# V projected and sent out ahead of Q and K in each of a kernel's eight attentions

## The chip, the core and the metric

The kernel runs on one core of a Trainium2 chip. The metric is the device time of one execution in microseconds (us); less is better. The five engines of the core run their own instruction streams and wait for each other on semaphores: TensorE (PE, matmuls), VectorE (DVE), ScalarE (ACT), GpSimd (POOL) and SyncE (SP), which here only issues DMAs. ACT issues DMAs as well.

## What is computed

Eight sequences of 512 tokens with 128 features go through four residual blocks, each behind a layer norm:

```python
x = x + ssm(layernorm(x))          # depthwise conv, state-space scan over time
x = x + ffn(layernorm(x))          # 8 experts, all computed, mixed by two softmaxes
x = x + attention(layernorm(x))    # below
x = x + ffn(layernorm(x))          # the same weights again

# attention: 16 heads of 8 features, chunk 10, left context 25
q = (x @ Wq.T + bq) * scaling;  k = x @ Wk.T + bk;  v = x @ Wv.T + bv
scores = q @ k.T + chunk_mask
out = softmax(scores) @ v
out = out @ Wo.T + bo
```

A query sees only its own chunk of 10 tokens and 25 to the left, so scores are computed for windows of 30 queries and 64 keys.

## The kernel before

**The beat.** The expert network is the bulk of the work. It is cut into 512 chunks (16 passes over a sequence, 32 chunks each; a chunk is 128 hidden features of one expert). In chunk `c` PE computes the gate projection `pg` (3 matmuls of 128x512, one line each of `split3`), the up projection `pu` of chunk `c-1` (3 more), and the down projections `pd` (line 994) of chunk `c-4` and its neighbours; ACT applies SiLU to `pg` (line 1049), DVE multiplies by `pu` (line 1087) and adds each finished expert into `x` (line 1075, "weigh").

**The side work.** The other blocks of other sequences are slipped between the chunks. Each is a generator per engine that yields the chunk at which its next piece is due, and `interleave` writes the pieces into that engine's stream in this order. A whole number is due after the chunk's `pg` and `pu` and ahead of its `pd`, a half number behind `pd`. So the order on each engine is fixed when the program is built, and the engines meet only at semaphores. `T_ATT[j] = 38 + 55 * j` is the chunk at which attention `j` begins, `T_SSM` holds the slots of the state-space blocks.

**An attention before its first scores.** PE transposes the normed rows (slot `t0 + 4`), ACT and DVE split them into two parts `axh`, `axl`. Then PE projects Q and K (slot 6, three matmuls of 128x512 each), and later V (slot 7.5, twelve matmuls of 128x128). They go to two PSUM banks in turn (`att_ps`): `take` waits until the bank's last user has freed it. ACT writes the high part of Q and K (line 720, slot 6.5), DVE the low part (line 754, slot 7), which frees the bank. DVE copies V into a padded layout `staged` (line 764, sixteen copies, slot 8), which frees V's bank.

**The DMAs of an attention, all in SP's queue** (q1 in the profile), in this order before the change:
- four stores of Q and K, high and low, to `qk_rows` in DRAM (line 836, 256 KB each), each behind its own producer;
- eight loads back into `q3` and `k3` in a regrouped layout (line 842, 256 KB each), each behind its store's landing;
- one store of V to `v_rows` (line 849, 1024 KB);
- eight gathers of V for the first half of the windows (line 863, 144 or 128 KB each, in pieces of 512 bytes), behind the landing of the V store; eight more for the second half, behind the scores of unit 1.

POOL builds the query weights for the first scores (line 886). It waits for all eight loads, for V's bank and for the V store:

```python
pool.wait_ge(qk_moved, 16 * 8 * (j + 1))
ab.wait_free(pool, ("v", j))
pool.wait_ge(v_out, 16 * (j + 1))
```

PE's first scores (line 676, slot `13.5 + 1/8`) wait for POOL's first two query weights, and everything behind them in PE's stream waits too.

**The state-space block's DMAs go through ACT's queue** (q10): per block eight loads of 256 KB (`arena<-bc_spread`, lines 607 and 611), each of which spreads 2 rows of DRAM over 128 partitions. POOL (lines 628, 632) uses them. Attentions 0, 2 and 4 have such loads in flight while their own DMAs run; the others have none at that point, or only at its end.

Of the kernel before, what the change touches and what calls it, by code (L numbers as in the profile page):

```python
# [8 lines left out]
F32 = mybir.dt.float32  # L9
# [4 lines left out]
B, L, D = 8, 512, 128  # L14
# [67 lines left out]
def build(nc, x_d, pack_d, wg_d, wu_d, wd_d, out_d):  # L82
    ctx = contextlib.ExitStack()
    with ctx:
# [558 lines left out]
        class Att:  # L643
# [9 lines left out]
            def pe(pe, link, j):  # L653
# [4 lines left out]
                ab.wait_free(pe, ("ln3", j))  # L658
                for w, name in ((wq, ("q", j)), (wk, ("k", j))):
                    ps = ab.take(pe, name)  # L660
                    ab.fill(split3(ps[:, :], [v[:, :] for v in w], (axh[:, 0:L], axl[:, 0:L])), name)
                yield t0 + 7.5
                ps = ab.take(pe, ("v", j))
                for t in range(TT):
# [3 lines left out]
                    last = nc.tensor.matmul(out, xw[0], wv[1][:, :], start=False, stop=True)  # L668
                ab.fill(last, ("v", j))

                def scores(n):
# [40 lines left out]
            def act(act, link, j):  # L712
# [3 lines left out]
                nc.scalar.copy(axh[:, 0:L], ab.ps(("ln3", j))[:, :]).then_inc(x_hi, 1)  # L716
                yield t0 + 6.5
                for w, v in enumerate("qk"):
# [21 lines left out]
            def dve(dve, link, j):  # L740
# [10 lines left out]
                yield t0 + 7  # L751
                for w, v in enumerate("qk"):
                    dve.wait_ge(qk_hi, 2 * j + w + 1)
                    ab.free(nc.vector.scalar_tensor_tensor(qk_s[:, w, 1, :], ab.ps((v, j))[:, :], pk("b_" + v),
                                                           qk_s[:, w, 0, :].bitcast(F32), ALU.add, ALU.subtract), (v, j))
                yield t0 + 8
                ab.wait(dve, ("v", j))
# [3 lines left out]
                for t in range(TT):  # L761

                    for r in range(4):
                        ins = nc.vector.tensor_copy(v_s[:, t, r, :].rearrange("p (g h d) -> p g h d", g=4, d=HD)[:, :, r, :],
                                                    ab.ps(("v", j))[:, t * P:(t + 1) * P]
                                                    .rearrange("p (g h d) -> p g h d", g=4, d=HD)[:, :, r, :])
                        if (t, r) == (TT - 1, 3):
                            ab.free(ins, ("v", j))
                        else:
                            link.count(ins)  # L770

                def masked(n):
# [49 lines left out]
            def sp(sp, link, j):  # L822


                qk_r = qk_d[j % 2]
                yield T_ATT[j] + 7
                if j >= 2:
                    sp.wait_ge(qk_moved, 16 * 8 * (j - 1))
                for w, v in enumerate("qk"):
                    for part in range(2):  # L830
                        yield T_ATT[j] + 7 + 0.5 * w
                        if part == 0:
                            sp.wait_ge(qk_hi, 2 * j + w + 1)
                        else:
                            ab.wait_free(sp, (v, j))
                        sp.dma_start(qk_r[w, part], qk_s[:, w, part, :].bitcast(F32)).then_inc(qk_out[w][part], 16)
                yield T_ATT[j] + 8
                for w, (dst, parts) in enumerate(((q3, (0, 0, 1, 1)), (k3, (0, 1, 0, 1)))):
                    for i, part in enumerate(parts):
# [3 lines left out]
                                     qk_r[w, part].rearrange("(g e) l -> e g l", g=4)).then_inc(qk_moved, 16)  # L843

                yield T_ATT[j] + 9
                if j:
                    sp.wait_ge(v_moved[1], 16 * 8 * j)
                ab.wait_free(sp, ("v", j))
                sp.dma_start(v_d[LEFT:LEFT + L, :].rearrange("(t p) x -> p t x", p=P), u_b[:, :, :]).then_inc(v_out, 16)

# [373 lines left out]
```

## Time and profile before

| | us |
|---|---|
| three runs | 1535.48, 1539.36, 1539.65 (median 1539.36) |
| the profiled execution, its own time | 1539.28 |
| its span from first to last instruction | 1537.5 |
| busy in it: PE | 1428.3 (93%) |
| DVE | 1000.8 (65%) |
| ACT | 791.9 (52%) |
| POOL | 459.5 (30%) |

Times in the rows are microseconds from the start of the span. "busy" counts instructions only, not waits and not the issuing of DMAs. Brackets behind a row of the timeline give how long the engine had stood idle before it and what released it. PEclk is the granted TensorE clock as a share of full speed (2.4 GHz); 0.50 is 1.2 GHz. "DMA share" is the mean busy share of the core's 16 DMA engines, so that 0.125 is what two busy engines make.

### The profile page before, as it was taken

The numbers are of one execution on the slowest core, as the hardware profiler recorded it, in microseconds if no ns is written. First come the engines' busy times: TensorE is split into PE (matmuls) and PEld (weight loads), VectorE is DVE, ScalarE is ACT, GpSimd is POOL, SyncE is SP. The second block draws the span as 40 slices with busy tenths as digits, with TensorE's granted clock in tenths as the row PEclk, the third lists the DMA queues.
The fourth block names the chain that finished last, engine by engine and source line by source line (L and its number), as shares of the span: only waits on it lengthen the run. The fifth ranks groups of instructions, "written<-read, shape, count | busy, mean of one in ns | idle before, by whom it ended". The sixth has DMA issues, their size and how long they took to land.

```text
span 1537.5 us, 27266 instructions
## 1 busy us (share of the span) xinstructions
PE 1428.3 (93%) x10580; PEld 1227.8 (80%) x10580; DVE 1000.8 (65%) x2317; ACT 791.9 (52%) x1114; POOL 459.5 (30%) x416
## 2 busy tenths in 40 slices
PE   5789957999999989999999899999999999999998
PEld 3577846887888878788788788887888888888887
DVE  5655636777587666866876577658756776486543
ACT  6462723855467445674656456465742555366321
POOL 4342253234232342223621354115512221141000
PEclk9999977999999999999999899999999999999999
DMA  5110142001601151014200520034004200420000
GB/s 171 45 47 23 55 139 45 15 16 49 155 1 36 45 141 25 2 43 151 45 8 10 169 47 22 1 129 83 28 1 132 44 1 2 138 38 2 1 7 8
DMA packets 82076, 81.57 MB, mean 53 GB/s; under 512 B 4748, under 2 KB 55948, under 8 KB 81948
## 3 DMA queue, kind: packets, MB, share of 16 engines
q1 hardware_dynamic: 74444, 64.92, 15.8%
q10 hardware_dynamic: 7504, 14.91, 2.7%
q8 instruction: 84, 1.38, 0.4%
q14 instruction: 44, 0.36, 0.1%
HBM read 60.65 MB, written 19.17 MB: 52 GB/s over the span
## 4 chain that ended last, share of the span: by engine, by line
PE 69%; DVE 11%; DMA 7%; issue 5%; ACT 5%; POOL 3%; SPq 1%; ACTq 0%; DVEq 0%; POOLq 0%
PE pd L994 23%; PE pg L270 7%; PE pu L270 6%; PE pg L272 6%; PE pg L271 6%; PE pu L271 6%; PE pu L272 6%; DMA arena<-bc_spread 3%; PE att_ps L676 3%; DVE h L1087 2%; PE att_ps L698 1%; DMA v_rows<-staged 1%; DVE x L1075 1%; DMA att_arena<-v_rows 1%; DVE att_arena L798 1%
## 5 line engine op out<-in xcount | busy, mean ns | idle before, releaser
L1049 ACT ACTIVATE h<-pg 128x512 f32<-128x512 f32 x512 | 304.0, 598 | 631.2 <-PE pg L272 620.6
L994 PEld LDWEIGHTS pd<-w_down,h 128*128 128x128 f32 x4096 | 513.7, 193 | 31.1 <-issue 3.9
L994 PE MATMUL pd<-w_down,h 128*128 128x128 f32 x4096 | 533.2, 279 | 1.1 <-DVE x L1075 1.1
L1087 DVE TENSOR_TENSOR h<-h,pu 128x512 f32<-128x512 f32 x512 | 344.0, 676 | 207.2 <-PE pu L272 206.1
L270 PE MATMUL pg<-ffn_x_hi,w_gate_hi 128*128 128x512 f32 x512 | 246.2, 481 | 5.4 <-ACT h L1049 3.9
L270 PE MATMUL pu<-ffn_x_hi,w_up_hi 128*128 128x512 f32 x512 | 208.2, 407 | 27.4 <-DVE h L1087 27.3
L271 PE MATMUL pu<-ffn_x_lo,w_up_hi 128*128 128x512 f32 x512 | 205.5, 401 | 0.0
L271 PE MATMUL pg<-ffn_x_lo,w_gate_hi 128*128 128x512 f32 x512 | 205.4, 401 | 0.0
L272 PE MATMUL pg<-ffn_x_hi,w_gate_lo 128*128 128x512 f32 x512 | 205.0, 400 | 0.0
L272 PE MATMUL pu<-ffn_x_hi,w_up_lo 128*128 128x512 f32 x512 | 204.8, 400 | 0.0
L899 POOL TENSOR_TENSOR att_arena<-att_arena 128x512 f32<-128x512 f32 (+1 forms) x72 | 73.8, 1025 | 352.9 <-DVE att_arena L789 352.9
L886 POOL TENSOR_TENSOR q_weights<-q,pack 128x512 fp32r<-128x512 f32 x136 | 145.1, 1088 | 102.6 <-DMA v_rows<-staged 102.5
L1049 ACT ACT_TABLE_LOAD x124 | 159.1, 1283 | 8.4 <-issue 6.2
L1075 DVE SCALAR_TENSOR_TENSOR x<-pd,mix,x 128x128 f32<-128x128 f32 x512 | 143.5, 342 | 22.2 <-PE pd L994 18.1
L270 PEld LDWEIGHTS pu<-ffn_x_hi,w_up_hi 128*128 128x128 f32 x512 | 97.8, 191 | 59.8 <-DVE h L1087 36.9
L272 PEld LDWEIGHTS pg<-ffn_x_hi,w_gate_lo 128*128 128x128 f32 x512 | 98.3, 192 | 24.1
L272 PEld LDWEIGHTS pu<-ffn_x_hi,w_up_lo 128*128 128x128 f32 x512 | 97.9, 191 | 24.2
L271 PEld LDWEIGHTS pu<-ffn_x_lo,w_up_hi 128*128 128x128 f32 x512 | 98.1, 192 | 22.8
L270 PEld LDWEIGHTS pg<-ffn_x_hi,w_gate_hi 128*128 128x128 f32 x512 | 99.9, 195 | 13.3 <-ACT h L1049 5.0
L271 PEld LDWEIGHTS pg<-ffn_x_lo,w_gate_hi 128*128 128x128 f32 x512 | 99.9, 195 | 4.8 <-issue 1.4
L676 PEld LDWEIGHTS att_ps<-k,q_weights 128*128 128x128 f32 x544 | 74.3, 199 | 27.6 <-issue 21.9
L676 PE MATMUL att_ps<-k,q_weights 128*128 128x64 f32 x544 | 70.7, 274 | 20.6 <-POOL q_weights L886 20.6
(189 smaller groups left out, 1472.6 us busy)
## 6 DMA issues: line engine op xcount, KB each, us to landing
arena<-bc_spread ACTq DMA_DIRECT2D x56, 256.0 KB
att_arena<-v_rows SPq DMA_DIRECT2D x64, 144.0 KB, 4.0
qk_rows<-qk_parts SPq DMA_DIRECT2D x32, 256.0 KB, 3.0
q<-qk_rows SPq DMA_DIRECT2D x32, 256.0 KB, 3.7
k<-qk_rows SPq DMA_DIRECT2D x32, 256.0 KB, 4.7
v_rows<-staged SPq DMA_DIRECT2D x8, 1024.0 KB, 8.5
att_arena<-v_rows SPq DMA_DIRECT2D x64, 128.0 KB, 4.1
arena<-in_x SPq DMA_DIRECT2D x8, 256.0 KB, 2.9
```

What stands on the lines that cost most here:

```text
L270: nc.tensor.matmul(out, w[0], x_parts[0], start=first, stop=False)
L271: nc.tensor.matmul(out, w[0], x_parts[1], start=False, stop=False)
L272: return nc.tensor.matmul(out, w[1], x_parts[0], start=False, stop=last)
L676: last = nc.tensor.matmul(ps[:, (4 * i + g) * WK:(4 * i + g + 1) * WK], q_w[:, n % 2, i, g, :, :].rearrange("p r q -> p (r q)"), k3[:, g, ...
L698: last = nc.tensor.matmul(ps[32 * g:32 * g + 32, i * QW:(i + 1) * QW], v_w[:, w, v, 32 * g:32 * g + 32], pt[n % 2][:, i, g, v, :], start=( ...
L798: link(nc.vector.tensor_tensor(u, u, rs.unsqueeze(3).broadcast_to([P, nw, 4, WK]), ALU.mult))
L886: nc.gpsimd.tensor_tensor(q_w[:, n % 2, i, :, :, :], q3[:, :, w * WQ:w * WQ + QW].bitcast(F32).unsqueeze(2) .broadcast_to([P, 4, 4, QW]), ...
L899: nc.gpsimd.tensor_tensor(u, u, smax[:, 0:nw, :].unsqueeze(3).broadcast_to([P, nw, 4, WK]), ALU.subtract).then_inc(s_sub, 1)
L994: last = nc.tensor.matmul(pd[:, t * P:(t + 1) * P], h_b[:, d % NH, t * P:(t + 1) * P], wd[:, d % NCH, :], start=d % CPE == 0 and t == 0, s ...
L1049: nc.scalar.activation(h_b[:, c % NH, :], pg[c % 2][:, :], ACT.Silu).then_inc(gate_done, 1)
L1075: nc.vector.scalar_tensor_tensor(x[:, t, :], pd[:, t * P:(t + 1) * P], mix[m % 2][:, t, e % E:e % E + 1], x[:, t, :], ALU.mult, ALU.add).t ...
L1087: nc.vector.tensor_tensor(h, h, pu[d % 2][:, :], ALU.mult).then_inc(h_done, 1)
```

## The change

In each attention V now goes first. On PE the twelve V matmuls stand at slot 6 and Q and K at slot 7. DVE's copies of V stand at slot 7 and its low parts of Q and K at slot 8; ACT's high parts move from 6.5 to 7.5. In SP's queue the store of V stands ahead of the stores and loads of Q and K. No instruction is added, removed or resized, and no semaphore that anyone waits for is changed. POOL's code and order are the same.

```diff
@@ PE
                 ab.wait_free(pe, ("ln3", j))
-                for w, name in ((wq, ("q", j)), (wk, ("k", j))):
-                    ps = ab.take(pe, name)
-                    ab.fill(split3(ps[:, :], [v[:, :] for v in w], (axh[:, 0:L], axl[:, 0:L])), name)
-                yield t0 + 7.5
                 ps = ab.take(pe, ("v", j))
...
                 ab.fill(last, ("v", j))
+                yield t0 + 7
+                for w, name in ((wq, ("q", j)), (wk, ("k", j))):
+                    ps = ab.take(pe, name)
+                    ab.fill(split3(ps[:, :], [v[:, :] for v in w], (axh[:, 0:L], axl[:, 0:L])), name)
@@ ACT
-                yield t0 + 6.5
+                yield t0 + 7.5
                 for w, v in enumerate("qk"):
@@ DVE
                 yield t0 + 7
-                for w, v in enumerate("qk"):
-                    dve.wait_ge(qk_hi, 2 * j + w + 1)
-                    ab.free(nc.vector.scalar_tensor_tensor(qk_s[:, w, 1, :], ab.ps((v, j))[:, :], pk("b_" + v),
-                                                           qk_s[:, w, 0, :].bitcast(F32), ALU.add, ALU.subtract), (v, j))
-                yield t0 + 8
                 ab.wait(dve, ("v", j))
...
+                yield t0 + 8
+                for w, v in enumerate("qk"):
+                    dve.wait_ge(qk_hi, 2 * j + w + 1)
+                    ab.free(nc.vector.scalar_tensor_tensor(qk_s[:, w, 1, :], ab.ps((v, j))[:, :], pk("b_" + v),
+                                                           qk_s[:, w, 0, :].bitcast(F32), ALU.add, ALU.subtract), (v, j))
@@ SP
+                yield T_ATT[j] + 7
+                if j:
+                    sp.wait_ge(v_moved[1], 16 * 8 * j)
+                ab.wait_free(sp, ("v", j))
+                sp.dma_start(v_d[LEFT:LEFT + L, :].rearrange("(t p) x -> p t x", p=P), u_b[:, :, :]).then_inc(v_out, 16)
                 qk_r = qk_d[j % 2]
-                yield T_ATT[j] + 7
+                yield T_ATT[j] + 8
...
-                yield T_ATT[j] + 9
-                if j:
-                    sp.wait_ge(v_moved[1], 16 * 8 * j)
-                ab.wait_free(sp, ("v", j))
-                sp.dma_start(v_d[LEFT:LEFT + L, :].rearrange("(t p) x -> p t x", p=P), u_b[:, :, :]).then_inc(v_out, 16)
```

The order of SP's issues around attention 0; the rows with a minus are those of before (line 849 is the V store), those with a plus those of the change (line 830 is the V store, 842 the stores and 848 the loads of Q and K).

```order
 L913 DMA arena<-in_x 128x4x128
 L917 DMA x<-in_x 128x4x128
-L836 DMA qk_rows<-qk_parts 128x512 x4
-L842 DMA q<-qk_rows 32x4x512 x4
-L842 DMA k<-qk_rows 32x4x512 x4
-L849 DMA v_rows<-staged 128x4x512
+L830 DMA v_rows<-staged 128x4x512
+L842 DMA qk_rows<-qk_parts 128x512 x4
+L848 DMA q<-qk_rows 32x4x512 x4
+L848 DMA k<-qk_rows 32x4x512 x4
 L863 DMA att_arena<-v_rows 32x8x128 x8
 L913 DMA arena<-in_x 128x4x128
```

The V store has passed twelve other DMAs, and the last thing in front of the gathers is now a load of K instead of the store of V.

The order on PE in attention 1, first of before, from K's projection to the first two V matmuls:

```order
L270 MATMUL att_ps<-attn_x,w_k_hi 128x512
L271 MATMUL att_ps<-attn_x,w_k_hi 128x512
L272 MATMUL att_ps<-attn_x,w_k_lo 128x512
L994 MATMUL pd<-w_down,h 128x128 x4
L270 MATMUL pg<-ffn_x_hi,w_gate_hi 128x512
L271 MATMUL pg<-ffn_x_lo,w_gate_hi 128x512
L272 MATMUL pg<-ffn_x_hi,w_gate_lo 128x512
L270 MATMUL pu<-ffn_x_hi,w_up_hi 128x512
L271 MATMUL pu<-ffn_x_lo,w_up_hi 128x512
L272 MATMUL pu<-ffn_x_hi,w_up_lo 128x512
L666 MATMUL att_ps<-w_v_hi,attn_x 128x128
L667 MATMUL att_ps<-w_v_hi,attn_x 128x128
```

and of the change at the same place, from the last V matmul to K's first:

```order
L664 MATMUL att_ps<-w_v_lo,attn_x 128x128
L994 MATMUL pd<-w_down,h 128x128 x4
L270 MATMUL pg<-ffn_x_hi,w_gate_hi 128x512
L271 MATMUL pg<-ffn_x_lo,w_gate_hi 128x512
L272 MATMUL pg<-ffn_x_hi,w_gate_lo 128x512
L270 MATMUL pu<-ffn_x_hi,w_up_hi 128x512
L271 MATMUL pu<-ffn_x_lo,w_up_hi 128x512
L272 MATMUL pu<-ffn_x_hi,w_up_lo 128x512
L270 MATMUL att_ps<-attn_x,w_q_hi 128x512
L271 MATMUL att_ps<-attn_x,w_q_hi 128x512
L272 MATMUL att_ps<-attn_x,w_q_lo 128x512
L270 MATMUL att_ps<-attn_x,w_k_hi 128x512
```

V has taken the place of Q and K, and Q and K stand one chunk's `pd`, `pg` and `pu` behind it. The second bank used after V is Q's; K comes back to V's.

The order on DVE at the same attention, with the high parts of Q and K awaited by lines 754 (before) and 769 (change):

```order
 L1087 TENSOR_TENSOR h<-h,pu 128x512 x2
 L1075 SCALAR_TENSOR_TENSOR x<-pd,mix,x 128x128 x4
-L754 SCALAR_TENSOR_TENSOR qk_parts<-att_ps,pack,qk_parts 128x512 x2
-L1087 TENSOR_TENSOR h<-h,pu 128x512
-L764 COPY staged<-att_ps 128x4x8 x16
+L759 COPY staged<-att_ps 128x4x8 x16
+L1087 TENSOR_TENSOR h<-h,pu 128x512
+L769 SCALAR_TENSOR_TENSOR qk_parts<-att_ps,pack,qk_parts 128x512 x2
```

The sixteen copies and the two low parts have changed places around one product of the expert network.

## Rows read from the trace of the kernel before

**Rows 1.** The page: busy time of each engine

```profile
PE 1428.3 (93%) x10580; PEld 1227.8 (80%) x10580; DVE 1000.8 (65%) x2317; ACT 791.9 (52%) x1114; POOL 459.5 (30%) x416
```

**Rows 2.** Waits over the whole span: us in total, times, longest us

```profile
PE att_ps L676 <- POOL q_weights L886: 20.6, 3, 9.3
POOL q_weights L886 <- DMA v_rows<-staged: 102.5, 6, 29.9
```

**Rows 3.** Timeline of SP's DMA issues, attention 2: start, us, line, tile, count

```profile
534.04 2.07 SPq L836 DMA_DIRECT2D qk_rows<-qk_parts  x4
...
544.88 0.64 SPq L849 DMA_DIRECT2D v_rows<-staged  x1
556.26 20.65 SPq L863 DMA_DIRECT2D att_arena<-v_rows  x16
```

**Rows 4.** Timeline of POOL and PE at the first scores, attentions 2 and 4

```profile
556.40 2.04 POOL L886 TENSOR_TENSOR q_weights<-q,pack 128x512 fp32r<-128x512 f32 x2 [10.11 <-DMA v_rows<-staged]
...
558.58 1.89 PE L676 MATMUL att_ps<-k,q_weights 128*128 128x64 f32 x8 [4.62 <-POOL q_weights L886]
...
875.80 3.51 POOL L886 TENSOR_TENSOR q_weights<-q,pack 128x512 fp32r<-128x512 f32 x2
...
879.45 1.89 PE L676 MATMUL att_ps<-k,q_weights 128*128 128x64 f32 x8 [6.67 <-POOL q_weights L886]
```

**Rows 5.** Windows: stretch, length, busy us of each engine, PEclk, DMA share, GB/s

```profile
484.00:488.00 4.00, 4.00 (x54) 3.27 (x54) 3.51 (x8) 3.46 (x5) 2.34 (x2) 1.00 0.13 49
...
552.00:556.00 4.00, 1.96 (x11) 1.34 (x10) 0.00 (x0) 1.84 (x3) 0.00 (x0) 1.00 0.14 54
...
871.00:875.00 4.00, 1.78 (x10) 1.16 (x8) 0.00 (x0) 0.60 (x1) 0.57 (x1) 1.00 0.13 51
```

**Rows 6.** Timeline of SP's DMA issues, attention 6

```profile
1171.44 2.09 SPq L836 DMA_DIRECT2D qk_rows<-qk_parts  x4
...
1180.27 0.54 SPq L849 DMA_DIRECT2D v_rows<-staged  x1
1186.45 3.79 SPq L863 DMA_DIRECT2D att_arena<-v_rows  x8
```

**Rows 7.** Windows of attention 6: its stores and loads, then the gathers

```profile
1173.00:1185.00 12.00, 12.00 (x81) 10.79 (x80) 8.47 (x36) 3.44 (x7) 2.52 (x3) 1.00 0.95 325
...
1187.00:1193.00 6.00, 6.00 (x43) 5.45 (x43) 2.49 (x8) 1.87 (x3) 3.64 (x4) 1.00 0.95 176
```

**Rows 8.** Timeline of POOL and PE at the first scores, attentions 5, 6 and 7

```profile
1033.17 4.04 POOL L886 TENSOR_TENSOR q_weights<-q,pack 128x512 fp32r<-128x512 f32 x4 [29.89 <-DMA v_rows<-staged]
...
1035.58 0.97 PE L676 MATMUL att_ps<-k,q_weights 128*128 128x64 f32 x8
...
1192.21 0.97 PE L676 MATMUL att_ps<-k,q_weights 128*128 128x64 f32 x8
...
1333.82 4.04 POOL L886 TENSOR_TENSOR q_weights<-q,pack 128x512 fp32r<-128x512 f32 x4 [25.77 <-DMA v_rows<-staged]
...
1336.80 0.97 PE L676 MATMUL att_ps<-k,q_weights 128*128 128x64 f32 x8
```

**Rows 9.** Timeline of PE and DVE around the projections, attentions 1 and 0

```profile
378.52 0.40 PE L270 MATMUL att_ps<-attn_x,w_k_hi 128*128 128x512 f32 x1
...
379.22 1.05 PE L994 MATMUL pd<-w_down,h 128*128 128x128 f32 x8
...
380.31 1.13 DVE L1075 SCALAR_TENSOR_TENSOR x<-pd,mix,x 128x128 f32<-128x128 f32 x4 [1.54 <-PE pd L994]
...
382.15 0.33 PE L666 MATMUL att_ps<-w_v_hi,attn_x 128*128 128x128 f32 x1 [0.47 <-DVE qk_parts L754]
...
190.95 1.65 DVE L764 COPY staged<-att_ps 128x32 f32<-128x32 f32 x16
```

**Rows 10.** Timeline of POOL, attention 0

```profile
221.62 1.26 POOL L628 TENSOR_TENSOR arena<-arena 128x512 f32<-128x512 f32 x1 [3.49 <-DMA arena<-bc_spread]
222.83 2.48 POOL L886 TENSOR_TENSOR q_weights<-q,pack 128x512 fp32r<-128x512 f32 x2
```

More of the change, by code:

```diff
@@ L830, in sp @@
                     for part in range(2):
-                        yield T_ATT[j] + 7 + 0.5 * w
+                        yield T_ATT[j] + 8 + 0.5 * w
                         if part == 0:
@@ L836, in sp @@
                         sp.dma_start(qk_r[w, part], qk_s[:, w, part, :].bitcast(F32)).then_inc(qk_out[w][part], 16)
-                yield T_ATT[j] + 8
+                yield T_ATT[j] + 9
                 for w, (dst, parts) in enumerate(((q3, (0, 0, 1, 1)), (k3, (0, 1, 0, 1)))):
```

## The prediction

> **What bounds the kernel now.** The page comes first: PE is busy for 1428.3 us of the span of 1537.5, 93% [rows 1]. So anything that PE does not wait for is worth little here, and the question is which of PE's waits the change touches. The table of waits is read next. PE waits 20.6 us, in three places, for POOL's query weights ahead of an attention's first scores, and POOL in turn waits 102.5 us in six places for the landing of V's store [rows 2]. That is the place at which the change aims. The timelines then say what the six are worth. In attention 2 SP issues the V store last, at 544.88; it lands at 556.26, when the gathers go out [rows 3]; POOL starts at 556.40 and PE's scores at 558.58, after 4.62 us idle [rows 4]. Attention 4 is alike: POOL at 875.80, PE idle for 6.67 us [rows 4]. The third place, 9.3 us [rows 2], is attention 0, and it is no V wait: POOL waited until 221.62 for a load of the state-space block, and did the query weights only behind it [rows 10]. In attentions 5, 6 and 7 PE does not wait at all [rows 8]. So the V store costs PE time in attentions 2 and 4 only, 11.3 us together, and that is the most that this place can give back.
>
> **Why it lands so late.** The windows tell. In 552 to 556 and 871 to 875, the last 4 us before these landings, the DMA share is 0.14 and 0.13, and 54 and 51 GB/s move [rows 5]. That is 2 engines of 16. The stretch 484 to 488, in which only the state-space block's loads run, has the same share, 0.13, and 49 GB/s [rows 5]. I read it so: these loads run on two engines, at some 25 GB/s each; what SP issues is spread over all 16, 14 are done early, and the landing waits for the two that serve both queues. The Trainium skill, page "DMA: Bandwidth & Descriptors", section "Why a DMA increments its semaphore by 16 and not by 1", has a rule of this kind: a transfer uses the largest number of engines up to 16 that divides the slowest dimension on both sides, and the lowest-numbered ones. A source of 2 rows would get 2 engines; the trace agrees, with its 0.13.
>
> **The part that is moved in the DMA queue.** Ahead of POOL's release SP moves 4 x 256 KB of stores, 8 x 256 KB of loads and 1024 KB of V: 4.2 MB, or 0.26 MB for each engine. On a shared engine that is 10.5 us at 25 GB/s, and about twice that while the other queue takes turns; from 534.04 to 556.26 [rows 3] are 22.2 us. The sum of bytes is the same in any order, and POOL waits for all of it, before and after. If the two engines never run dry, the release comes when they have done 0.26 MB each, and only the start counts. They stayed busy before, since each group of issues left before the last had drained. After the change they should stay busy too: V's 1024 KB cover the time until the stores of Q and K land and their loads can go out. So V's landing comes earlier, and that of the last load of K takes its place.
> - The start: V's matmuls stand where those of Q and K stood, but the first store now has to wait for DVE's sixteen copies, 1.65 us [rows 9], where before it needed one high part on ACT. It is later by 0 to 1.65 us. The high part that it replaces took time as well, so I take 0.6 each in attentions 2 and 4, 1.2 us, range 0 to 3.3.
> - Attentions without the other queue: in attention 6 the first store left at 1171.44 and V landed at 1186.45 [rows 6], with 325 GB/s at share 0.95 in between [rows 7]; data flowed some 1.5 us after the issue. Now: issue at 1173.1, flow from 1174.6, 4.2 MB by 325 GB/s is 12.9 us, landing 1.45 us behind (1185 to 1186.45): 1189.0, or 2.5 us later. Two of POOL's four query weights take half of 4.04 us [rows 8], so PE would be served at 1191.2, and comes at 1192.21 [rows 8]: nothing. Attention 5 has 0.4 us to spare by the same sum (1033.17 + 2.02 against 1035.58), attention 7 1.0 us [rows 8]. Moved by 2.5 us they would cost 2.1 and 1.5. I take 0.8 for both, as their stores left with gaps that V now fills; range 0 to 3.6.
> - Attention 0: the cover is the chain of the state-space loads that ends at 221.62 [rows 10]. It stays hidden while these come last. They share two engines with the same bytes as before: 0, between -1 and +2.
>
> **The gathers.** They wait for V's landing, and behind it in SP's queue for nothing new. They now follow the last load of K at once, near 546 in attention 2, where they left at 556.26 [rows 3]. PE hardly waits for them, so no gain. But they run on 14 engines while the two shared ones still drain. Their pieces of 512 bytes move 176 GB/s at the same share, 0.95, at which the pieces of 2 KB move 325 [rows 7]. If what slows them is common to all engines, the two are slowed to 0.54 for the 4 us of the window [rows 5]: 1.8 us in each of attentions 2 and 4. If it is each engine's own, 0. I take 0.5 each, 1.0 us, nearer to the lower end, as each ring works its pieces for itself. The Trainium skill, in the table at the head of the same page, gives 512 bytes as the least transfer for line rate. By that rule this term would be 0 and the sum 1.0 us smaller; the trace does not bear it out, with 176 against 325.
>
> **The PSUM banks on PE.** Before, V's first matmul waited for the low part of Q, 0.47 us in attention 1 [rows 9]. Now K waits for V's bank, that is for all sixteen copies. In attention 1 DVE ends its work on `x`, which waits for the `pd` at 379.22, at 381.44 [rows 9]; with 1.65 us of copies the bank is free at 383.1. PE, which stood there ready at 381.68 before [rows 9], has Q's three matmuls to do first (as long as K's, 378.52 to 379.22 [rows 9], 0.7 us) and comes at 382.4: it waits 0.7 instead of 0.47. Such a thing can happen wherever a DVE item stands ahead of the copies, in three attentions by the order of before: 0.7 us in all, range 0 to 3. DVE's low parts, ACT's high parts one chunk later, and POOL's part have cover: the loads come out of the queue behind V's bytes anyhow. Would that cover go, the slot of one chunk, 2.3 to 3 us, would be the price in attentions 2 and 4.
>
> **Sum.** 1.2 + 0.8 + 0 + 1.0 + 0.7 = 3.7 us. The profiled execution took 1539.28 us (its span is 1537.5; 1.8 lie around it), 0.1 below the median of the three runs. That gives **1543.0 us**, 0.24% more than before.
>
> **The rivals.**
> - Faster: the last landing comes sooner. On a shared engine V's 65 KB took 5.2 us at half of 25 GB/s. If the V store fills time in which the two engines stood idle for SP's queue, the loads land where they did, and POOL is released 5.2 us sooner: 4.6 us less in attention 2, all of its wait, and 5.2 in attention 4, 9.8 us: 1529.5. For it: stores and loads are a round trip with a wait for landings in it. Against it: 22.2 us for 10.5 us of work leave no idle stretch when half goes to the other queue. Chance 0.15.
> - Slower, by the gathers: all 16 engines share what slows them. Then the 1.8 us of attentions 2 and 4 come whole, and as much of attention 0's chain: 5.5 us in place of 1.0, 1547.5. It decides from 1.9 us on, where the sum passes 0.3%. For it: 176 against 325 GB/s. Against it: the gathers are only moved, and the load that POOL awaits in attention 0 has less beside it later. Chance 0.22.
> - No change in effect: V lands early, all else comes as before, no one is later: 1539.3. For it: small terms all. Chance 0.12.
> - My forecast, 1540.5 to 1546: chance 0.46. The last 0.05 is for what I have not named.
>
> **The numbers.** 0.3%, 4.6 us, is about what a measurement of this kernel can tell from no change. Faster by more: 0.15 and 0.02 of the unnamed, 0.17. Slower by more: the gathers' 0.22 and about a quarter of my own case, 0.35. The rest, 0.48, is the same. The range leaves out the faster case's centre and reaches its upper part, 1532, and above takes in the gathers' case with the upper bounds of starts and banks, 1552. My own case alone has 1540 to 1546.
>
> **What would show it.** V's store is issued near 534.6 in attention 2 and lands some 8 us later; POOL's query weights still start within 2 us of 556.4 plus any shift of all before, now released by a load of K; PE's wait there is 4.6 to 6 us, and 6.7 to 8 in attention 4. The window ahead of the release still shows a share near 0.13, or more with the gathers in it. PE's K projection shows waits for DVE's copies under 1 us. In attention 6 POOL is released about 2.5 us later and PE waits for nothing. I am wrong if POOL's release in attentions 2 and 4 moves ahead by several us, if attention 0's third wait changes by more than 2 us, or if the attentions without the other queue begin to stall PE.

## The result, and the profile after

| | median us | runs | ratio to before |
|---|---|---|---|
| before | 1539.4 | 1535.5 to 1540.2 | |
| changed | 1548.5 | 1541.9 to 1551.7 | 1.006, interval 1.0035 to 1.0085 |
| changed, measured again | 1550.1 | 1543.7 to 1552.3 | 1.0066, interval 1.0041 to 1.009 |

The change makes the kernel 9 to 10 us slower by the ratios. (The medians of the second measurement differ by 12.6. The ratio comes with an interval and is taken as the firmer number; where the two disagree, both are given.) The forecast was 1543.0, slower by 0.24%. The profile shown here is of the fastest of the first five executions, 1541.92 us, so that it shows only part of the loss.

The page of the changed kernel, its span and busy times:

```profile
span 1540.1 us, 27266 instructions
...
PE 1425.1 (93%) x10580; PEld 1223.5 (79%) x10580; DVE 999.8 (65%) x2317; ACT 793.2 (52%) x1114; POOL 458.2 (30%) x416
```

PE has no more work than in [rows 1]; it stands idle longer, 115.0 us (the span less its busy time) against 109.2. The table of its waits, us in total, times, longest, against [rows 2]:

```profile
PE att_ps L676 <- POOL q_weights L886: 28.9, 5, 11.5
...
PE att_ps L270 <- DVE staged L759: 1.4, 2, 0.7
```

The wait for the query weights has grown from 20.6 us in three places to 28.9 in five. The timelines of attentions 2, 4, 5 and 6 at the first scores, for [rows 4] and [rows 8]; brackets hold PE's or POOL's idle time and what ended it:

```profile
555.85 2.04 POOL L886 TENSOR_TENSOR q_weights<-q,pack 128x512 fp32r<-128x512 f32 x2 [12.92 <-DMA k<-qk_rows]
...
558.03 1.89 PE L676 MATMUL att_ps<-k,q_weights 128*128 128x64 f32 x8 [6.45 <-POOL q_weights L886]
...
878.89 2.04 POOL L886 TENSOR_TENSOR q_weights<-q,pack 128x512 fp32r<-128x512 f32 x2 [6.72 <-DMA k<-qk_rows]
...
881.07 1.89 PE L676 MATMUL att_ps<-k,q_weights 128*128 128x64 f32 x8 [9.02 <-POOL q_weights L886]
...
1038.08 1.05 PE L676 MATMUL att_ps<-k,q_weights 128*128 128x64 f32 x8 [0.78 <-POOL q_weights L886]
...
1194.79 1.05 PE L676 MATMUL att_ps<-k,q_weights 128*128 128x64 f32 x8 [1.18 <-POOL q_weights L886]
```

POOL is now released by a load of K, not by V's store. PE waits 6.45 and 9.02 us where it waited 4.62 and 6.67, and in attentions 5 and 6, where it did not wait, 0.78 and 1.18. SP's issues in attentions 4 and 6, for [rows 6]:

```profile
854.02 0.36 SPq L830 DMA_DIRECT2D v_rows<-staged  x1
855.19 3.73 SPq L842 DMA_DIRECT2D qk_rows<-qk_parts  x4
...
863.01 2.75 SPq L848 DMA_DIRECT2D k<-qk_rows  x4
865.86 32.82 SPq L863 DMA_DIRECT2D att_arena<-v_rows  x16
...
1173.96 0.38 SPq L830 DMA_DIRECT2D v_rows<-staged  x1
1176.03 5.27 SPq L842 DMA_DIRECT2D qk_rows<-qk_parts  x4
...
1186.56 4.34 SPq L863 DMA_DIRECT2D att_arena<-v_rows  x8
```

The gathers of V leave at 865.86, 13 us ahead of POOL's release at 878.89, and at 1186.56 in attention 6, 6 us ahead of it (1192.60). Before, they left with the release. In attention 6 that release now comes 21.9 us after the first projection of the attention, where it came after 16.8. The windows (length, busy times, PEclk, DMA share, GB/s), for [rows 5] and [rows 7]:

```profile
552.00:556.00 4.00, 0.00 (x0) 0.00 (x0) 0.00 (x0) 0.00 (x0) 0.15 (x1) 0.96 0.46 104
874.00:878.00 4.00, 0.00 (x0) 0.00 (x0) 1.84 (x6) 0.00 (x0) 0.00 (x0) 0.82 0.13 50
1177.00:1183.00 6.00, 6.00 (x38) 5.21 (x37) 5.06 (x16) 1.80 (x3) 2.33 (x3) 1.00 0.63 226
```

The stretch of two busy engines is still there in attention 4 (share 0.13). In attention 2 the gathers fill it (0.46 instead of 0.14). In attention 6 the engines are not full while the stores of Q and K go out: 0.63.

### The profile page after: what moved, and what is told of

Its sections match the earlier page's. It is cut to its first block, busy times and chain, and to the rows that moved or that the text cites. A ratio compares the mean times of both kernels' runs of the same rounds, so it can differ in the third digit from the quotient of the medians.

```text
span 1540.1 us, 27266 instructions
## 1 busy us (share of the span) xinstructions
PE 1425.1 (93%) x10580; PEld 1223.5 (79%) x10580; DVE 999.8 (65%) x2317; ACT 793.2 (52%) x1114; POOL 458.2 (30%) x416
## 4 chain that ended last, share of the span: by engine, by line
PE 67%; DVE 12%; DMA 6%; issue 6%; ACT 5%; POOL 4%; SPq 1%; ACTq 0%; DVEq 0%; POOLq 0%
PE pd L994 23%; PE pg L270 6%; PE pu L270 6%; PE pg L272 6%; PE pg L271 6%; PE pu L271 6%; PE pu L272 6%; DMA arena<-bc_spread 4%; PE att_ps L676 3%; DVE h L1087 2%; PE att_ps L698 1%; DVE x L1075 1%; POOL arena L626 1%; POOL arena L628 1%; DMA k<-qk_rows 1%
## 5 line engine op out<-in xcount | busy, mean ns | idle before, releaser
L1075 DVE SCALAR_TENSOR_TENSOR x<-pd,mix,x 128x128 f32<-128x128 f32 x512 | 143.6, 343 | 24.9 <-PE pd L994 20.6
L270 PEld LDWEIGHTS pg<-ffn_x_hi,w_gate_hi 128*128 128x128 f32 x512 | 99.4, 194 | 12.8 <-ACT h L1049 4.8
L676 PE MATMUL att_ps<-k,q_weights 128*128 128x64 f32 x544 | 70.8, 274 | 28.9 <-POOL q_weights L886 28.9
```

The lines of the kernel that those rows point to most:

```text
L270: nc.tensor.matmul(out, w[0], x_parts[0], start=first, stop=False)
L676: last = nc.tensor.matmul(ps[:, (4 * i + g) * WK:(4 * i + g + 1) * WK], q_w[:, n % 2, i, g, :, :].rearrange("p r q -> p (r q)"), k3[:, g, ...
L1075: nc.vector.scalar_tensor_tensor(x[:, t, :], pd[:, t * P:(t + 1) * P], mix[m % 2][:, t, e % E:e % E + 1], x[:, t, :], ALU.mult, ALU.add).t ...
```

## The experiments

There are two theories. **A: the early gathers.** V's landing comes early, so the gathers leave ahead of the landing of the loads of Q and K, and slow these. **B: the late projections.** Q and K are projected a chunk later, their stores leave later, and V's store ahead of them does not make up for it. Each run below was timed beside the kernel before; times are medians.

**The changed kernel again.** No edit.

> The changed kernel once more, unaltered, to learn how far its executions spread and whether the stretches of its first profile recur. That profile is of a run of 1541.9 us, the fastest of five with a median of 1548.5. All theories expect a median of 1544 to 1550, a ratio of 1.003 to 1.008 and waits of PE for the query weights of 27 to 38 us in the table of waits (28.9 in the first profile, 20.6 before). If the profile is of a slower run, the theory of early gathers expects the extra time in attentions 0, 2 and 4, the theory of late low parts in attentions 5, 6 and 7.

Measured: 1550.1 us against 1537.4 of before. Its profile (1549.8 us) has waits as the first had: 30.0 us for the query weights, in five places. The extra time is not in one attention: counted from each attention's first projection, POOL reached the query weights 3 to 4 us later than before in attentions 1, 2, 3, 4 and 6 (in attention 3, 20.8 us against 17.2), though only those with too little slack make PE wait. Which ones do changes between executions: besides 0, 2 and 4 they are attentions 5 and 6 in the first profile, 3 (1.61 us) and 5 (0.16) in this one. Of its 10.5 us over the profile before, 6.3 are idle time of PE and 4.2 are longer matmul time, at a mean granted clock of 0.965 against 0.977. The run told the theories apart no further, but it gives the spread: executions of this kernel differ by 9 us.

**The gathers held back.** The changed kernel, with one wait more:

```diff
                     if half_w == 0:
                         yield T_ATT[j] + 12
+                        sp.wait_ge(qk_moved, 16 * 8 * (j + 1))
                         sp.wait_ge(v_out, 16 * (j + 1))
```

> The changed kernel, with one more wait in SP's queue: the first half of the gathers of V leaves only when all loads of Q and K have landed. Theory A (early gathers slow the two shared engines while they drain): in attentions 2 and 4 POOL's release comes 1.5 to 3 us sooner after V's projection than the 26.8 and 28.1 us of the changed kernel, the windows of the last 4 us ahead of it show a DMA share of 0.13 again, and the time falls by 4 to 8 us against the changed kernel, to about 1542. Theory B (the stores and loads of Q and K simply leave later): the release stays where it is within 1 us, and the time too.

Measured: **1538.0 us**, ratio to before 1.0004, interval 0.999 to 1.0019: the loss is gone. Against the changed kernel, measured beside it, that is 12.1 us by the medians and 9.5 by the ratios. The timeline of attention 4 in the changed kernel (second measurement):

```profile
869.45 2.82 SPq L848 DMA_DIRECT2D k<-qk_rows  x4
872.37 12.79 SPq L863 DMA_DIRECT2D att_arena<-v_rows  x8
...
885.60 2.04 POOL L886 TENSOR_TENSOR q_weights<-q,pack 128x512 fp32r<-128x512 f32 x2 [6.01 <-DMA k<-qk_rows]
```

its wait for the query weights in the table of waits:

```profile
PE att_ps L676 <- POOL q_weights L886: 30.0, 5, 11.6
```

the same timeline with the gathers held:

```profile
867.47 2.65 SPq L848 DMA_DIRECT2D k<-qk_rows  x4
881.20 18.80 SPq L864 DMA_DIRECT2D att_arena<-v_rows  x14
...
881.25 2.04 POOL L887 TENSOR_TENSOR q_weights<-q,pack 128x512 fp32r<-128x512 f32 x2 [5.77 <-DMA k<-qk_rows]
```

and the wait:

```profile
PE att_ps L676 <- POOL q_weights L887: 23.0, 3, 10.6
```

From the end of the last load's issue to POOL's release are 13.3 us with the early gathers (872.27 to 885.60) and 11.1 without (870.12 to 881.25). In attention 1, where the last load of the state-space block was issued more than 20 us before, the same is seen, first with the early gathers, then with the gathers held:

```profile
391.20 2.88 SPq L848 DMA_DIRECT2D k<-qk_rows  x4
...
399.30 3.04 POOL L886 TENSOR_TENSOR q_weights<-q,pack 128x512 fp32r<-128x512 f32 x3 [20.01 <-DMA k<-qk_rows]
```

```profile
391.11 2.89 SPq L848 DMA_DIRECT2D k<-qk_rows  x4
...
397.62 4.04 POOL L887 TENSOR_TENSOR q_weights<-q,pack 128x512 fp32r<-128x512 f32 x4 [18.42 <-DMA k<-qk_rows]
```

The same stretch is 5.2 us (394.08 to 399.30) and 3.6 (394.00 to 397.62). The PE wait falls from 30.0 to 23.0 us, and PE's whole idle time from 115.5 to 106.8. This held profile is of the slowest of twelve executions of its kernel (1544.1), and PE is busy 3.0 us longer in it for the same matmuls; so the two profiles differ by 5.7 us where the medians differ by 12.1. Where the rest lies, they do not show. That the early gathers cost the whole loss is shown, and what theory B expected, the release and the time where they were, is refuted. The gain was larger than the 4 to 8 us that theory A expected from attentions 2 and 4.

**The engines' order alone.** PE, ACT and DVE as changed, SP's queue as before (V's store behind the loads of Q and K). The edit puts the old body of `Att.sp` back into the changed kernel.

```diff
-                yield T_ATT[j] + 7
-                if j:
-                    sp.wait_ge(v_moved[1], 16 * 8 * j)
-                ab.wait_free(sp, ("v", j))
-                sp.dma_start(v_d[LEFT:LEFT + L, :].rearrange("(t p) x -> p t x", p=P), u_b[:, :, :]).then_inc(v_out, 16)
                 qk_r = qk_d[j % 2]
...
+                yield T_ATT[j] + 9
+                if j:
+                    sp.wait_ge(v_moved[1], 16 * 8 * j)
+                ab.wait_free(sp, ("v", j))
+                sp.dma_start(v_d[LEFT:LEFT + L, :].rearrange("(t p) x -> p t x", p=P), u_b[:, :, :]).then_inc(v_out, 16)
```

> The changed kernel's order on PE, ACT and DVE, with SP's queue in the old order (stores and loads of Q and K, then V's store). Theory B (what costs is that Q and K are projected a chunk later, and V's store ahead of them only fills the time): the stores of Q and K leave 3 to 4 us later than before, V behind them, POOL's release comes 3 to 4 us later than before in every attention, and PE begins to wait in attentions 3, 5, 6 and 7: 12 to 16 us over before, 1552 to 1555, so worse than the changed kernel. Theory A (SP's order with the early gathers costs): near the kernel before, 1539 to 1543.

Measured: 1554.1 us, 16.6 over before, as theory B had it. The waits:

```profile
POOL q_weights L886 <- DMA v_rows<-staged: 124.8, 7, 30.6
PE att_ps L676 <- POOL q_weights L886: 33.4, 7, 10.8
```

PE waits in seven attentions. So the late projections do cost, and V's place at the head of SP's queue is worth as much: 1554.1 against 1538.0 with the gathers held in both (here they wait for V, which is last). By the medians the change is 16.6 us lost by the late Q and K, 16.1 won by the early V store, and 12.1 lost by the gathers that it sets free; by the ratios it is 15.1, 14.5 and 9.5.

**The low parts half a chunk earlier.** In the changed kernel's DVE part:

```diff
-                yield t0 + 8
+                yield t0 + 7.5
                 for w, v in enumerate("qk"):
                     dve.wait_ge(qk_hi, 2 * j + w + 1)
```

> The changed kernel, with DVE's low parts of Q and K due half a chunk sooner (slot 7.5 for 8), so that they stand ahead of the next chunk's product and of the adding of an expert into x. Theory B, in its sharper form (in the changed kernel SP's four stores of Q and K are stretched over 5.3 us in attention 6, because the low parts stand behind the adding of an expert, and the DMA engines run dry meanwhile, share 0.63 in 1177 to 1183): the four stores leave within 3 us, the release in attention 6 comes 1.5 to 2.5 us sooner after V's projection than the 21.9 us of the changed kernel, in attentions 2 and 4 up to 1 us, and the time falls by 2 to 4 us. Theory A: no change beyond 1 us.

Measured: 1547.6 us, ratio 1.0064, 0.9 us below the first measurement of the changed kernel and 2.5 below the second, no difference that can be told. Its waits:

```profile
PE pu L270 <- DVE h L1087: 30.6, 23, 5.9
PE att_ps L676 <- POOL q_weights L886: 27.8, 5, 11.5
```

In attention 6 the release did come about 2 us sooner (18.8 us after the first projection, where the second measurement has 20.6), and the wait for the query weights is 2.2 us less than the 30.0 of the changed kernel. But the product of the expert network now stands behind the low parts, and PE's wait for it is 30.6 us instead of 26.6. In the sum of the two waits nothing is gained.

**The query weights in memory of their own.** An edit of the kernel before. The query weights share memory with the padded V, which is why POOL has to wait for V's store:

```diff
-        with contextlib.ExitStack() as shared:
-            q_w = shared.enter_context(nc.sbuf_tensor("q_weights", [P, 2, 2, 4, 4, QW], F32R))
+        q_w = sb("q_weights", [P, 2, 2, 4, 4, QW], F32R)
...
-                pool.wait_ge(v_out, 16 * (j + 1))
...
                         ab.wait(pool, ("s", j - 1, NUNIT - 1))
+                        pool.wait_ge(v_out, 16 * j)
```

> The kernel before, with the query weights in memory of their own (before, they share it with the padded V), so that POOL need not wait for the landing of V's store ahead of them; that wait is moved to POOL's clearing of the padded V of the next attention. It measures by itself what the landing of V costs. If it is worth what the timelines say, POOL's release in attentions 2 and 4 comes 5 us sooner, PE's wait there falls from 4.6 and 6.7 us to 0 and 1.6, and the time falls by 8 to 11 us, to about 1530. If the bytes alone set it (the two shared engines), the loads land at the same time as before and the same gain appears, since V's bytes are last in the queue. If PE merely meets another wait a few chunks later: less than 4 us.

Measured: 1533.7 us, ratio 0.9966, interval 0.9954 to 0.9979: 4.8 us faster, half of what was expected if the timelines were right. Timeline of attentions 2 and 4:

```profile
552.65 2.04 POOL L884 TENSOR_TENSOR q_weights<-q,pack 128x512 fp32r<-128x512 f32 x2 [5.59 <-DMA k<-qk_rows]
...
872.47 1.26 POOL L627 TENSOR_TENSOR arena<-arena 128x512 f32<-128x512 f32 x1 [4.40 <-DMA arena<-bc_spread]
873.68 2.48 POOL L884 TENSOR_TENSOR q_weights<-q,pack 128x512 fp32r<-128x512 f32 x2
...
876.31 1.89 PE L675 MATMUL att_ps<-k,q_weights 128*128 128x64 f32 x8 [4.44 <-POOL q_weights L884]
```

Attention 2's wait is gone. In attention 4 POOL reaches the query weights only behind a product for the state-space block, which waits for a load on the other queue: 4.44 us of PE's 6.67 remain. The next wait in POOL's order took the place of the first. Elsewhere PE waits longer for DVE's product (`pu <- h`), 32.0 us in all against 27.3 before.

**The state-space loads split in two.** An edit of the kernel before, for `btile` and likewise for `ctile`, with POOL's waits doubled from 16 to 32:

```diff
-                    act.dma_start(btile[k % 2], bc_r[2 * k:2 * k + 2, :].unsqueeze(1)
-                                 .broadcast_to([2, INNER, L])).then_inc(b_moved[k % 2], 16)
+                    for r in range(2):
+                        act.dma_start(btile[k % 2][r * INNER:(r + 1) * INNER, :], bc_r[2 * k + r:2 * k + r + 1, :]
+                                      .broadcast_to([INNER, L])).then_inc(b_moved[k % 2], 16)
```

> The kernel before, with each load of the state-space block (2 rows spread over 128 partitions) issued as two loads of one row over 64 partitions, which by the reading of the windows should run on all 16 DMA engines instead of 2. The reading that two shared engines set the landings: the windows ahead of the release lose their stretch of share 0.13, V's store lands 4 to 7 us sooner in attentions 2 and 4, and in attention 0 the load that POOL awaited until 221.6 comes 10 us sooner or more; PE's wait for the query weights falls from 20.6 us to under 6, ACT is no longer held up while issuing; ACT pays 0.5 us for each of 56 more issues. Time 1515 to 1528. If the loads still take two engines: no gain, up to 10 us slower for the issues.

Measured: **1491.4 us**, ratio 0.9692, interval 0.968 to 0.9705: 47 us faster than before, twice the upper end of what was expected. The page:

```profile
span 1488.9 us, 27322 instructions
...
arena<-bc_spread ACTq DMA_DIRECT2D x112, 128.0 KB, 2.9
```

Its table of waits:

```profile
PE att_ps L679 <- POOL q_weights L889: 4.0, 2, 2.6
...
PE pu L270 <- DVE h L1090: 15.1, 16, 2.1
```

Three windows (columns as in those above): 4 us while attention 0's V store was on its way,

```profile
186.00:190.00 4.00, 4.00 (x24) 3.35 (x24) 1.70 (x3) 2.66 (x4) 3.84 (x3) 1.00 1.00 355
```

the same for attention 4, and 2 us in which only two of the split loads were on their way:

```profile
830.00:834.00 4.00, 4.00 (x25) 3.49 (x24) 1.10 (x2) 2.58 (x4) 3.21 (x2) 1.00 0.81 309
...
271.00:273.00 2.00, 2.00 (x15) 1.73 (x13) 1.90 (x5) 1.97 (x3) 0.32 (x1) 1.00 0.36 131
```

No wait of POOL for a state-space load is among the first sixty rows of the table of waits any more; before, they were 80.6 us. A load lands 2.9 us after its issue in the median, the stretch of share 0.13 ahead of the release is gone (0.81, 309 GB/s in attention 4), and PE's wait for the query weights is 4.0 us instead of 20.6. The reading that two engines served these loads and held up the landings beside them is borne out.

The 47 us are not all at the place under study. By the start of each attention's first projection, this profile is 12.4 us ahead before attention 0 begins. It gains 19.2 more by attention 1, 5.2 in and behind attention 2, 8.0 in and behind attention 4, and 3.9 in and behind attention 5; the spans differ by 48.6. In attention 0 a second thing was at work. In the kernel before, two of ACT's issues of these loads held ACT up, and the SiLU of the expert network with it:

```profile
192.25 8.50 ACTq L607 DMA_DIRECT2D arena<-bc_spread  x1
...
201.02 9.06 ACTq L611 DMA_DIRECT2D arena<-bc_spread  x1
```

With the split no pair of issues takes more than 1.9 us. Of the 48.6 us, 34.1 are less idle time of PE, and 14.5 are shorter busy time for the same matmuls (1413.8 us against 1428.3), at a mean granted clock of 0.991 against 0.977.

**The changed order with the split, and with the split and held gathers.** The two edits above on the changed kernel.

> The changed kernel with the same split of the state-space block's loads. Without the two shared engines theory A has nothing left to slow, so it expects the changed order to cost at most 1 us against the kernel before with the same split. Theory B expects the release to come later than with the old order by the start alone, 1.5 to 3.5 us in each attention, which costs PE only where its slack is smaller: 1 to 5 us over the other split kernel.

> The changed kernel with the split loads of the state-space block (1503.8 us) and, on top, the gathers of V held back until all loads of Q and K have landed. The kernel before with the same split took 1491.4. Theory A in its new form (early gathers slow whatever runs beside them on any engine, not just the two shared ones): holding them gives back most of the 12.3 us here as well, 1491 to 1495. Theory B (Q and K a chunk later, whose cost showed as 16.6 us with the engines' order alone): 1500 to 1504, as the gathers have no two slow engines to slow.

Measured: 1503.8 us with the split alone, 12.3 over the old order with the same split; 1495.6 with the gathers held as well, 4.1 over it. By the ratios to before (0.9781, 0.9729 and 0.9692) the two differences are 13.7 and 5.7 us. PE's wait for the query weights in the two, one row of each:

```profile
PE att_ps L679 <- POOL q_weights L889: 11.3, 6, 3.5
```

```profile
PE att_ps L679 <- POOL q_weights L890: 5.5, 3, 2.4
```

The expectation that theory A has nothing left to slow once the two shared engines are gone was wrong, and 12.3 us is above theory B's 1 to 5 as well: early gathers cost 8.2 us here too. The slowing does not need two shared engines: from the end of the last load's issue to POOL's release, the stretch is 0.9 to 2.0 us longer with the early gathers in each of attentions 1 to 7, and the same in attention 0 (7.2 us). The other 4.1 us are what theory B has left.

**Idle traffic at the early place.** The changed kernel with held gathers, and at the early place eight gathers more into spare memory; then the same with pieces of 2 KB. Nothing computes with them; their landing is waited for only ahead of the next attention's V store.

```diff
                         sp.wait_ge(v_out, 16 * (j + 1))
+                        for r in range(4):
+                            for v in range(2):
+                                cols = v_d[32 * v:32 * v + 1, P * r:P * (r + 1)]
+                                sp.dma_start(spare[32 * r:32 * r + 32, :, v, :], ...).then_inc(idle, 16)
                         sp.wait_ge(qk_moved, 16 * 8 * (j + 1))
```

> The changed kernel with its gathers held (1538.0 us), and at the early place eight more gathers of the same pieces of 512 bytes into spare memory that nobody waits for until the next attention: the early traffic alone, 1 MB an attention more. Theory A: the release of POOL is again 1 to 2 us later in each attention, and the time is 1546 to 1556, at least that of the changed kernel, since the true gathers follow on top. If the early traffic is innocent and it was something else about the early issue: 1538 to 1541.

> As the run with the idle gathers, but the same 1 MB moved in 64 pieces of 2 KB by each of eight transfers. If it is the small pieces that cost (176 against 325 GB/s in the kernel before), the idle traffic takes half the time and costs at most half of what the idle gathers cost: 1540 to 1544. If bytes count and not pieces: the same time as with the idle gathers, within 2 us.

Measured: 1553.6 us with pieces of 512 bytes, 1558.5 with pieces of 2 KB. The waits of the first, and of the second:

```profile
PE att_ps L677 <- POOL q_weights L895: 27.6, 5, 11.3
...
PE att_ps L699 <- DMA att_arena<-v_rows: 9.0, 2, 7.7
```

```profile
PE att_ps L677 <- POOL q_weights L893: 32.0, 5, 13.9
...
PE att_ps L699 <- DMA att_arena<-v_rows: 5.2, 2, 3.2
```

The early traffic brings the longer wait for the query weights back: 27.6 and 32.0 us against 23.0. The slowing of the loads itself comes back in part only: from the end of the last load's issue to POOL's release are 12.5 and 12.8 us in attention 4 (11.1 with the gathers held, 13.3 with them early) and 9.5 and 9.7 in attention 2 (9.5 and 11.3). It also makes the true gathers late (9.0 and 5.2 us of PE waiting for them), a cost that the changed kernel does not have, so the 15.6 and 20.6 us over the held gathers' 1538.0 are not the price of early traffic alone. The second time fits neither thing that was expected, 1540 to 1544 or within 2 us of the first. But large pieces are no gentler than small ones, and the explanation by small pieces falls.

**Q and K half a chunk behind V.** On top of the held gathers:

```diff
-                yield t0 + 7
+                yield t0 + 6.5
                 for w, name in ((wq, ("q", j)), (wk, ("k", j))):
@@ ACT
-                yield t0 + 7.5
+                yield t0 + 7
@@ DVE
-                yield t0 + 8
+                yield t0 + 7.5
```

> The changed kernel with held gathers, and Q and K on PE due half a chunk after V instead of a whole one (slot 6.5 for 7), the high parts at 7 and the low parts at 7.5. Theory B: Q and K come 1.4 us sooner, the release too, and PE's waits for the query weights fall by 1 to 3 us in all; against that K may wait for V's bank up to 1.5 us more in each attention, which takes back up to 8 us. Net 1534 to 1544; below 1535 it would be the best version of this order. Theory A has no opinion beyond the 1538.0 of the held gathers.

Measured: 1543.7 us, ratio 1.0031, interval 1.0016 to 1.0046. The waits:

```profile
PE att_ps L676 <- POOL q_weights L887: 16.6, 3, 9.5
...
PE att_ps L270 <- DVE staged L759: 6.6, 4, 2.1
```

The wait for the query weights fell from 23.0 to 16.6 us, and PE waits 6.6 us for V's bank (1.4 with the gathers held alone), which took most of the gain back. This profile is of the fastest of twelve executions (1538.8), so the balance that it shows is kinder than the median. Why the median lies 5.7 us over the held gathers (4.2 by the ratios) it does not show.

**The best version.** The kernel before with split loads and the query weights in memory of their own.

> The kernel before with both the split loads and the query weights in memory of their own: the version that should beat both kernels. If each removes what the other leaves, PE's wait for the query weights is gone, and the time is that of the split alone less 0 to 5 us, 1512 to 1526.

Measured: 1490.0 us, ratio 0.9688, interval 0.9675 to 0.97. That is 1.5 us below the split alone, within what runs differ by, so it can't be told from it. It is 22 us below the range that was expected, since the split alone already was. No order with V first reached the two; the nearest took 1495.6.

## Why the prediction came out as it did

The direction was right, and the time within the range of 1532 to 1552; the size was some 0.3 to 0.4 of what was measured (3.7 us against 9 to 10 by the ratios, 12.6 by the medians of the second measurement). The range holds the result by its width: my own case alone had 1540 to 1546, and "slower by more than 0.3%", which is what came, had a chance of 0.35. Two of the named signs of being wrong came true: attentions without the other queue began to stall PE, and attention 0's third wait moved by more than 2 us (9.3 to 11.5). PE's wait in attentions 2 and 4 was 6.45 and 9.02 us, above the 4.6 to 6 and 6.7 to 8 of the forecast.

**What bounds, and why V lands late: right.** Two engines served the state-space loads and delayed what shared them; with the split the stretch of share 0.13 and 16.6 of PE's 20.6 us of waiting are gone. That these loads cost 47 us in all, far more than the place under study, I had not seen.

**Bytes in any order, only the start counts: right as far as it goes.** POOL was released by a load of K in V's place, and with the gathers held the kernel takes 1538.0 us, 0.6 over before, interval -1.5 to +2.9. The terms of start, attentions 5 to 7 and banks were 2.7 us together, inside it; that the sum comes out is in part luck, for its parts are larger: the engines' order costs 16.6 us and V's early store gives 16.1 back. K's wait for V's bank in attention 1 was forecast at 0.7 us:

```profile
380.52 0.50 PE L270 MATMUL att_ps<-attn_x,w_k_hi 128*128 128x512 f32 x1 [0.69 <-DVE staged L759]
```

**The step that failed is the term of the gathers**, "I take 0.5 each, 1.0 us, nearer to the lower end, as each ring works its pieces for itself". It was mis-sized: holding them back gave 12.1 us by the medians, 9.5 by the ratios. Three things in it were wrong. First, the 0.5 leaned to the lower end: with the gathers held, PE's wait is 2.0 us shorter in attention 2 (7.39 to 5.38) and 2.2 in attention 4, so the upper bound of 1.8 was about right there. That it was so is luck, since it came from the 4 us of a window that I had chosen, and the overlap is 13 us in attention 4. Second, the cost is not confined to attentions 2 and 4. Attention 0's wait is 1.1 us shorter with the gathers held, attention 3's 1.6, and 5 and 6 began to wait as well in the first profile. Third, I took it to need the two shared engines, but it is there also with all loads spread (8.2 us), and in attention 1, where no load of the other queue is on the way. The slower rival named the gathers and gave them 0.22 and 1547.5 us; it was the nearest to what came. Its argument by small pieces was not borne out. Its mechanism, something that all 16 engines share, is not shown either: pieces of the gathers that run on the same engines as the loads would do the same, and no run tells the two apart.

**The cover of the low parts: wrong, and at nothing in the sum.** Its price, one chunk or 2.3 to 3 us in attentions 2 and 4, stood only as a condition. They were to be hidden behind V's bytes; in attention 6 the four stores of Q and K stretched over 5.27 us and the share fell to 0.63. POOL's release there came 5.1 us later after the first projection, not 2.5, and PE, which was to wait for nothing, waited 1.18 us. Moving them forward changed the time by nothing that can be told, as PE then waited for the expert network's product.

**The faster rival fell:** V early did not release POOL early. Attention 0's third wait was forecast to stay; it rose from 9.3 to 11.5 us and fell back to 10.6 with the gathers held, so the range of -1 to +2 was slightly too narrow.

What stays open: how the early gathers slow the loads (2.2 us in attention 4's release, 1.6 in attention 1's) was not traced to a resource. And the two profiles account for only 5.7 us of the difference.

## What to carry to other kernels

An early landing sets free whatever waits for it. Before a store is moved ahead in a queue, look for the transfers behind it that its landing releases, and ask what they will run beside; if nobody needs them yet, hold them behind the transfers that somebody does.

A stretch with a DMA share of 2/16 while everyone waits is a sign to look at how each transfer is cut over the engines first: here that was worth 47 us, more than any order of the queue that was tried.

## What the runs showed of the hardware

A load of 2 DRAM rows spread over 128 partitions ran at a share of 0.13, that of two engines, and 49 GB/s [rows 5]. As two loads of one row over 64 partitions each, 128 KB landed in 2.9 us in the median, and in a stretch with only two such loads on the way the share was 0.36 at 131 GB/s. The Trainium skill, page "DMA: Bandwidth & Descriptors", section "Why a DMA increments its semaphore by 16 and not by 1", says that a DMA takes the largest number of engines up to 16 that divides the slowest dimension of both sides; with the slowest dimension 2 that is two engines, with 64 sixteen. The trace agrees with the first, by its 0.13; of the second it shows that more than two engines ran, by its 0.36, and not that all sixteen did.

In this kernel transfers queued behind others slowed these. With 1 MB of gathers right behind the loads of Q and K, POOL was released 13.3 us after the end of the last load's issue in attention 4, without them 11.1; in attention 1 it was 5.2 and 3.6.

An issue held up the engine that issued it. Most issues of a state-space load took ACT's queue 0.49 us; in attention 0 of the kernel before, where three others had been issued in the 12 us before, one took 8.50 and one 9.06 us, and ACT computed nothing for 6.35 and 6.20 us of it.
